# Cross attention with its softmax by blocks of 1024 keys, each block turned on TensorE and its two halves copied by ScalarE and VectorE

## What is computed

```python
x = x + _L0_xattn_ref(_layernorm(x, axis=-1), ctx_768, ctx_768, ...)
...
q = jnp.einsum('bqd,dh->bqh', query, Wq) + bq
k = jnp.einsum('bkd,dh->bkh', key, Wk) + bk
v = jnp.einsum('bkd,dh->bkh', value, Wv) + bv
scores = jnp.einsum('bqh,bkh->bqk', q, k)
weights = jax.nn.softmax(scores, axis=-1)
return jnp.einsum('bqk,bkh->bqh', weights, v)
```

```python
powers = jnp.exp(dtA[:, :, None] * jnp.arange(L))
K = 2.0 * jnp.einsum('dn,dnl->dl', dC, powers).real
```

## Time and profile before

| | us |
|---|---|
| median of 3 runs | 1661.75 (1659.3 to 1729.4) |
| the profiled execution | 1659.78 |
| its span | 1657.9 |
| mean granted TensorE clock | 0.933 of full speed |
| cross attention, first score pass to last output | 191.7 to 511.2 |

### The profile page before, as it was taken

One profiled execution on the slowest core, in us unless ns is written; L12 is line 12 of the kernel. 1 busy time (PEld: TensorE's weight loads), 2 busy tenths in 40 slices (PEclk: granted clock), 3 DMA queues, 4 the chain that ended last, 5 costly groups with the idle time before them and its releaser, 6 DMA issues. The chain is left out here.

```text
span 1657.9 us, 19830 instructions
## 1 busy us (share of the span) xinstructions
PE 1369.8 (83%) x6709; PEld 729.4 (44%) x6763; DVE 1255.7 (76%) x2833; ACT 897.2 (54%) x1424; POOL 678.3 (41%) x466
## 2 busy tenths in 40 slices
PE   6677699999997757889899988989875459999798
PEld 2223344333344434355555555555564323333465
DVE  5999567866515669999999999999878657776433
ACT  4666211457543320687778778877852146666311
POOL 2656111112101034688787878878861120000012
PEclk9799899999997878999999999999987759999899
DMA  6000011000005832000000000000040300000000
GB/s 152 1 0 1 28 58 49 0 1 0 1 0 125 174 103 63 1 1 1 1 1 1 1 1 1 1 1 1 7 152 1 89 1 1 1 1 1 1 0 14
DMA packets 32482, 42.99 MB, mean 26 GB/s; under 512 B 14286, under 2 KB 25644, under 8 KB 30992
## 3 DMA queue, kind: packets, MB, share of 16 engines
q1 hardware_dynamic: 29820, 29.61, 6.2%
q10 hardware_dynamic: 2552, 12.02, 3.5%
HBM read 33.48 MB, written 8.14 MB: 25 GB/s over the span
## 5 line engine op out<-in xcount | busy, mean ns | idle before, releaser
L1631 PE MATMUL psum<-film_ka,film_context_qa 97*128 97x427 bf16 (+3 forms) x896 | 329.8, 368 | 74.3 <-DVE film_stage_kept L1810 29.4
L2033 ACT ACTIVATE film_stage_e<-psum,film_stage_bias 128x512 f32<-128x512 f32 (+1 forms) x416 | 273.9, 668 | 96.9 <-PE psum L1633 87.0
L1810 DVE MAX8 film_stage_kept<-psum 128x8 f32<-128x213 f32 (+1 forms) x960 | 318.5, 377 | 6.6 <-PE psum L1633 6.3
L1633 PE MATMUL psum<-film_kb,film_context_qb 128*128 128x427 bf16 (+2 forms) x843 | 306.4, 364 | 0.0
L1882 POOL TENSOR_TENSOR film_stage_e<-film_stage_e 128x1024 f32<-128x1024 f32 (+1 forms) x91 | 207.1, 2276 | 80.7 <-DVE film_stage_e L1852 60.8
L1852 DVE SCALAR_TENSOR_TENSOR film_stage_e<-psum,film_context_top,film_stage_e 128x512 f32<-128x512 f32 (+1 forms) x325 | 231.8, 719 | 8.4 <-ACT film_stage_e L2033 6.7
L1631 PEld LDWEIGHTS psum<-film_ka,film_context_qa 97*128 97x128 bf16 x896 | 92.1, 103 | 195.3 <-DVE film_stage_kept L1810 86.8
L3235 POOL TENSOR_TENSOR residual<-residual,top_expert_kept 128x1024 f32<-128x1024 f32 x7 | 16.5, 2351 | 294.9 <-DVE top_expert_kept L3192 294.9
L1913 PEld LDWEIGHTS psum<-ctx_rows,film_stage_mean_T 128*128 128x128 f32 (+1 forms) x816 | 121.9, 192 | 30.0 <-issue 3.3
L2998 DVE TENSOR_REDUCE gqa_attend_low<-psum 128x1 f32<-128x128 f32 (+7 forms) x128 | 94.1, 755 | 43.1 <-PE psum L2917 40.7
L1913 PE MATMUL psum<-ctx_rows,film_stage_mean_T 128*128 128x96 f32 (+1 forms) x816 | 119.9, 269 | 1.8
(11 more groups left out here) (548 smaller groups left out, 2540.3 us busy)
## 6 DMA issues: line engine op xcount, KB each, us to landing
film_kb<-film_k_rows ACTq DMA_DIRECT2D x4, 1601.0 KB
film_ka<-film_k_rows ACTq DMA_DIRECT2D x3, 1601.0 KB
ctx_T<-in_ctx_T SPq DMA_DIRECT2D x1, 2401.5 KB
gqa_experts_w<-in_L_ffn_W SPq DMA_DIRECT2D x1, 2048.0 KB
film_stage_e<-in_dft_ahead SPq DMA_DIRECT2D x1, 1728.0 KB, 8.7
film_k_rows<-cross_attention_film_hi SPq DMA_DIRECT2D x6, 256.0 KB, 2.0
film_k_rows<-cross_attention_film_mid SPq DMA_DIRECT2D x6, 256.0 KB, 2.0
film_k_rows<-cross_attention_film_low SPq DMA_DIRECT2D x6, 256.0 KB, 2.0
```

The costliest lines, as they stand in the source:

```text
L1631: pe.matmul(out, a["qa"][0:ROWS, h, rows], a["ka"][0:ROWS, h, c + b:c + b + cols], start=True, stop=False)
L1633: last = pe.matmul(out, a["qb"][:, h, rows], a["kb"][:, h, c + b:c + b + cols], start=False, stop=True)
L1810: last = dve.max(kept[:, h % 2, PER_PIECE * u + s, :], bank[:, lo:hi])
L2033: act.activation(e[:, n % RING, sub, 0:PIECES[u][1]], ps[:, SEARCH_BANKS + q % WEIGH_BANKS, 0:PIECES[u][1]], ACT.Exp, bias=bias[:, i % 2, ...
```

## The change

The scores are formed once. For each block n = 7 i + c of 128 queries and 1024 keys, the loop over n (56 blocks and 4 iterations behind them) does this: TensorE forms the negative scores into one of two pairs of banks; VectorE takes their minimum per query; ScalarE takes exp(minimum - negative score) of 128x1024 into `prob`; two iterations later TensorE turns `prob` in two halves of four 128x128 tiles into banks 4 and 5; ScalarE copies the first half (h = 0) to `prob_T`, VectorE the second (h = 1); TensorE multiplies each turned tile as weights with 97 columns of `ctx_rows`, summed over the block in a place of its own in bank 6. The short block has a first half only. At the end of a row the seven minima give seven scales, and GpSimd scales and adds the seven sums. At the end the totals are turned and multiplied by `w_v` as before.

The S4D filter and the FiLM keys move into this loop. The FiLM keys are now 13 units of 512 columns, one in each iteration from 1 to 13, in bank 7 (`side`). The filter's small arithmetic is cut into parts 0 to 10, in the iterations 2 to 12 (`S4D_SMALL_AT`), the groups begin at iteration 12 (`S4D_FROM`), two of them every five iterations, and the filter's products, copies and turns use bank 7 too. The first loads of SyncE change places: those for keys and filter are issued ahead of the wait for `ones_set`.

In the diff below the helpers of the filter and the keys are left out; they are cut into pieces, but do the same operations, those of the keys on 512 columns.

```diff
+    LAG, PROBS, TURNED = 2, 3, 3
...
+    key_at = {KEYS_FIRST + u: u for u in range(len(KEY_UNITS))}
...
+    angles_at = {S4D_FROM + 5 * x // 4: divmod(x, 2) for x in range(2 * NG)}
+    pair_at = [S4D_FROM + 5 * p for p in range(NG // 2)]
+    scalar_at = {5: 1, 8: 2}
+    for p, n in enumerate(pair_at):
+        scalar_at[n + 4], scalar_at[n + 5] = 2 * p + 3, 2 * p + 4
+    decay_at = {n + 2 * b: 2 * p + b for p, n in enumerate(pair_at) for b in range(2)}
+    power_at = {n + 6 + b: 2 * p + b for p, n in enumerate(pair_at) for b in range(2)}
+    product_at = {n + 8 + b: 2 * p + b for p, n in enumerate(pair_at) for b in range(2)}
+    rows_at = {n + 10: p for p, n in enumerate(pair_at)}
...
+    END = max(BLOCKS + LAG + 2, max(kernel_at) + 1)
...
+    parts_at = {NB * i + FIRST_PART - 1 + LAG + 1: 2 * i for i in range(NT)}
+    parts_at.update({NB * (i + 1) - 1 + LAG + 1: 2 * i + 1 for i in range(NT)})
...
+            def bring_together(i):
+                pool.wait_ge(part_copied, 2 * i + 2)
+                pool.wait_ge(scale_ready, i + 1)
+                x = sums[:, i % 2]
+                link(pool.tensor_tensor(x, x, scale[:, i, :].unsqueeze(2).to_broadcast([P, NB, CA]), ALU.mult))
+                link(pool.tensor_tensor(x[:, 0:3], x[:, 0:3], x[:, 3:6], ALU.add))
+                link(pool.tensor_tensor(x[:, 0:2], x[:, 0:2], x[:, 2:7:4], ALU.add))
+                pool.tensor_tensor(total[:, i, :], x[:, 0], x[:, 1], ALU.add).then_inc(total_ready, 1)
...
+            def copy_turned(n, h):
+                k = half_at[n, h]
+                dve.wait_ge(turn_done, k + 1)
+                dve.tensor_copy(prob_T[:, k % TURNED, :], ps[:, 4 + k % 2, :]).then_inc(turned_high, 1)
...
+            for n in range(END):
+                if n in parts_at:
+                    copy_part(parts_at[n])
+                if n < BLOCKS:
+                    i, c = divmod(n, NB)
                     dve.wait_ge(score_done, n + 1)
...
-                    dve.reduce_max(tops[:, i, c:c + 1], pair(2 * (n % SCORE_PAIRS))[:, 0:width],
-                                   AX).then_inc(max_read, 1)
...
-            dve.wait_ge(max_read, NT * N_CHUNK)
-            link(dve.reduce_max(top[:], tops[:], AX))
-            dve.tensor_scalar(minus_top[:, :, DC], top[:], -1.0, None, ALU.mult).then_inc(top_ready, 1)
-            s4d_vector(dve, link, s4d, ps[:, 4, :])
...
+                    dve.tensor_reduce(shift[:, i, c:c + 1], scores(n), AX, ALU.min).then_inc(shift_ready, 1)
...
+                if (n - LAG, 1) in half_at:
+                    copy_turned(n - LAG, 1)
+                if n in key_at:
+                    film_key_vector(dve, film, side, key_at[n])
+                if n in small_at:
+                    s4d_vector_small(dve, link, s4d, side, small_at[n])
+                if n in angles_at:
+                    s4d_vector_angles(dve, link, s4d, *angles_at[n])
+                if n in power_at:
+                    s4d_vector_power(dve, s4d, power_at[n])
+            s4d_vector_skip(dve, link, s4d)
...
+            def turn(n, h):
+                k = half_at[n, h]
+                pe.wait_ge(prob_ready, n + 1)
+                if k >= 2:
+                    pe.wait_ge(*turned(k - 2))
+                for _, x, rows in key_tiles(n, h):
+                    last = pe.transpose(ps[0:rows, 4 + k % 2, x:x + P],
+                                        prob[:, n % PROBS, h * HALF + x:h * HALF + x + rows], g["ident"][:])
+                last.then_inc(turn_done, 1)
...
+            def weighted(n, h):
+                k = half_at[n, h]
...
+                pe.wait_ge(*turned(k))
+                if h == 0 and c in (0, FIRST_PART) and part >= 1:
+                    pe.wait_ge(part_copied, part)
+                for tile, x, rows in key_tiles(n, h):
+                    last = pe.matmul(ps[:, SUMS_BANK, place:place + CA], prob_T[0:rows, k % TURNED, x:x + P],
+                                     ctx[0:rows, tile, :], start=tile % 8 == 0,
+                                     stop=tile == min(8 * c + 7, KT - 1))
+                if (n, h + 1) not in half_at and c in (FIRST_PART - 1, NB - 1):
+                    last.then_inc(part_done, 1)
...
+            for n in range(END):
+                b = n - LAG
+                if 0 <= b < BLOCKS:
+                    turn(b, 0)
+                if 0 <= b - 1 < BLOCKS:
+                    weighted(*HALVES[half_at[b - 1, 0] + ((b - 1, 1) in half_at)])
+                if n < BLOCKS:
+                    i, c = divmod(n, NB)
+                    if n >= 2:
+                        pe.wait_ge(prob_ready, n - 1)
+                    for h in range(-(-width(n) // HALF)):
+                        cols = min(HALF, width(n) - h * HALF)
+                        last = pe.matmul(ps[:, 2 * (n % 2) + h, 0:cols], qc[:, i * P:(i + 1) * P],
+                                         ctx_T[:, c * CHUNK + h * HALF:c * CHUNK + h * HALF + cols],
+                                         start=True, stop=True)
+                    last.then_inc(score_done, 1)
+                if (b, 1) in half_at:
+                    turn(b, 1)
+                    weighted(b, 0)
+                if n in key_at:
+                    if key_at[n] == 0:
+                        pe.wait_ge(s4d["sem"]["zeroed"], 1)
+                    film_key_tensor(pe, film, ctx_T, side, key_at[n])
+                if n in product_at:
+                    if product_at[n] == 0:
+                        pe.wait_ge(film["sem"]["rest_ready"], len(KEY_UNITS))
+                    s4d_tensor(pe, s4d, side, product_at[n])
+                if n in turn_at:
+                    s4d_turn(pe, s4d, side, turn_at[n])
...
-            pe.wait_ge(shift_ready, 2)
...
-                for n in range(2):
-                    last = pe.matmul(ps[0:rows, 2 * (k % 2) + n, :], ctx_T[:, k * P:k * P + rows],
-                                     qc_shifted[:, n * HALF:(n + 1) * HALF], start=True, stop=True)
-                last.then_inc(prob_psum, 1)
-                if k >= 1:
-                    weighted(k - 1)
...
+            def copy_turned(n, h):
+                k = half_at[n, h]
+                act.wait_ge(turn_done, k + 1)
+                whole = sum(rows == P for _, _, rows in key_tiles(n, h)) * P
+                last = act.activation(prob_T[:, k % TURNED, 0:whole], ps[:, 4 + k % 2, 0:whole], ACT.Copy)
...
+            for n in range(END):
+                b = n - LAG
+                if (b, 0) in half_at:
+                    copy_turned(b, 0)
+                if n < BLOCKS:
+                    i, c = divmod(n, NB)
+                    act.wait_ge(shift_ready, n + 1)
+                    act.activation(prob[:, n % PROBS, 0:width(n)], scores(n), ACT.Exp, scale=-1.0,
+                                   bias=shift[:, i, c:c + 1]).then_inc(prob_ready, 1)
...
+                if n in key_at:
+                    film_key_high(act, film, side, key_at[n])
+                if n - 1 in key_at:
+                    film_key_middle(act, film, key_at[n - 1])
+                if n in scalar_at:
+                    s4d_scalar(act, s4d, scalar_at[n])
+                if n in rows_at:
+                    s4d_copy_rows(act, s4d, side, rows_at[n])
+                if n in kernel_at:
+                    s4d_copy_kernel(act, s4d, side, kernel_at[n])
+            for n in range(2):
```

More of the change, by code:

```diff
@@ L623, in s4d_vector, with s4d_vector_angles @@
+def s4d_vector_angles(dve, link, k, q, part):
+    sem = k["sem"]
+    b = q % RING_Q
+    group = slice(q * GROUP, (q + 1) * GROUP)
     i_index = k["index"][:, 0:P].unsqueeze(1).to_broadcast([P, GROUP, P])
-    for q in range(NG):
-        b = q % RING_Q
-        group = slice(q * GROUP, (q + 1) * GROUP)
+    if part == 0:
         if q >= RING_Q:
@@ L771, in film_key_store @@
     sem = f["sem"]
-    for u, (c, w) in enumerate(UNITS):
+    for u, (c, w) in enumerate(KEY_UNITS):
         for k, part in enumerate(("hi", "mid", "low")):
@@ L875, in cross_attention @@
     ctx_T = g["ctx_T"]
+    NB = N_CHUNK
+    BLOCKS = NT * NB
+    HALVES = [(n, h) for n in range(BLOCKS) for h in range(2) if h == 0 or n % NB < NB - 1]
+    half_at = {x: k for k, x in enumerate(HALVES)}
+    LAG, PROBS, TURNED = 2, 3, 3
+    FIRST_PART = 4
     w_q = m.sb("w_q", [P, D])
@@ new lines, in copy_part @@
+            def copy_part(part):
+                i = part // 2
+                blocks = part_blocks(part)
+                dve.wait_ge(part_done, part + 1)
+                if i >= 2:
+                    dve.wait_ge(total_ready, i - 1)
+                dve.tensor_copy(sums[:, i % 2, blocks[0]:blocks[-1] + 1, :],
+                                ps[:, SUMS_BANK, 0:len(blocks) * CA].rearrange("p (b c) -> p b c", c=CA)
+                                ).then_inc(part_copied, 1)
+            dve.memset(side, 0.0).then_inc(s4d["sem"]["zeroed"], 1)
@@ L1038, in _ @@
-            weighted(KT - 1)
-            pe.wait_ge(sum_ready, 1)
-            for i in range(NT):
```

(9 more changed lines are left out.)

425 lines of the change are left out of this document (200 added, 225 removed).

## The result

The changed kernel takes 1670.05 us (median of six runs, 1667.55 to 1672.61) where the kernel before takes 1661.97: ratio 1.0053, interval 1.0039 to 1.0067. It is 0.5% slower; I had forecast 0.8% less. The ratio leaves out one run of the kernel before (1729.4 us) that fell in the slower state of the chip. The profiled span went from 1657.9 to 1665.6 us. Where a place in a trace is compared between kernels, it is counted from the first reduction, which starts at 193.8 us here and between 193.2 and 197.3 in the traces of the experiments.

What follows compares the result with a forecast made beforehand. A ring through VectorE bounds the new loop, not TensorE's own work; 191.7 + 85 + 207 + 14 = 497.7 against 511.2, 13 us less, so 1649 us (-0.8%), range 1612 to 1680.

Steps and rivals of the forecast that it cites:

- The first 14 iterations: Iterations 0 to 13, which also carry the FiLM keys: 85 us, set by a round of 3.76 us plus small work.
- X: VectorE's small filter work added to the 3.76 us round in the first part: about 31 us with angles.
- port rival: GpSimd operations hold up VectorE's tensor_scalars: 39 us in all and 8 in the first part, kernel 1696; chance 0.06.
- The loop: Iterations 14 to 55, six rows: 34.5 us a row, of which 2.5 stick out of the ring's slack; 207 us.
- ScalarE's low copy: Iterations with sines and the next: copy delayed by 1.15 and 1.1 us, of which 0.65 and 0.6 are seen.
- The copy of the sums: VectorE's copies of the sums in each row: two copies, 0.3 us of a row's 32.
- the ring's idle 0.7: TensorE idle 0.7 us per full iteration (5.05 against 4.36 of work), covering 16 small filter matmuls of about 0.65.
- The end: Behind the last scores, through the last four of eight outputs (2.9 us): about 14 us, where 7.3 were.
- the ring through VectorE: Each score waits for VectorE's reduction, its high copy and that half's weighting: 5.05 us per full iteration.
- 41 and the turn: TensorE has 41 us less work in the sweeps, and the 5.1 us turn between them goes too.
- The clock: Rival: holes in each iteration lower TensorE's granted clock; at 0.85 28 us more, kernel 1677; chance 0.10.

Runs made afterwards that it cites:

- run 13: Changed kernel, but from the third key unit on GpSimd forms the low part of the keys on 8 columns, not 512: ratio 1.0005 to the kernel before.
- 9: Changed kernel, but GpSimd forms the decay of one channel in each group of eight, read by ScalarE for all eight: ratio 1.0023 to the kernel before.
- Runs 3: Changed kernel, with ScalarE's second filter step cut over two iterations, its exponential moved to the next: ratio 1.0067 to the kernel before.
- 10: Changed kernel, with sine and exponential of one index only in the filter's second step, table loads kept: ratio 1.0049 to the kernel before.
- run 6: Changed kernel, with VectorE also copying the low halves that ScalarE would copy behind its filter work (18 of 56): ratio 0.9996 to the kernel before.
- run 11: Changed kernel, with only two of the four key tiles in each full block's first half weighted: ratio 1.0012 to the kernel before.

## Why the prediction was wrong

**The step that failed** is the small work in "The first 14 iterations", 31 us for X: it measured 43.3 (38.6 and 4.7 of angles). I took it from a stretch of before in which the FiLM keys were done, and laid it beside GpSimd's low part, which I priced only as a store that is in time. I had its neighbour in hand: the earlier trace rows show the hold, and my port rival even wrote 8 us for the first part. But it was tied to the decays and given 0.06. The release decides: low part and small work are both freed within 0.05 us at the end of the same chain, so they meet in ten of thirteen units. By runs 13 and 9 the holds cost 8 us here and some 5 for the decays, where the rival had 39 for these: behind the power that frees a decay, a reduction and a copy out of PSUM come first in VectorE's queue, as at 317.4 and 344.4, and cover most of its 1.90 us. The Trainium skill ("SBUF — State Buffer", SBUF: two separate sides) tells of an exclusive lock; the held operations of run 13 and the unchanged reductions agree.

That 12.3 us of excess in X equal the first part's 12.2 is partly luck: with 8.6 of small work gone, run 13's first part is only 7.4 shorter.

**The other 4 to 5 us of the first part** hold the rest of the small work's excess, the second step (7.8 us waited), a sums copy behind VectorE's work (7.3), and the half clock behind these waits (about 5 us by the estimate above, so some other term must have been too long). Runs 3 and 10 show that shortening the step alone brings nothing, so its hole is not a separate price. I can't split it further.

**The loop**, 6.6 us. A row with nothing on top would be 3.43 + 6 x 4.79 = 32.2; I had 32. On top I had 2.5 a row, 14.6 us in 41 iterations; it is 20.1. Three terms were too small. ScalarE's low copy: I had 1.25 in five iterations, some 10, and TensorE waits 13.9, behind table load, two sines and the exponential in ScalarE's queue; run 6 gives back 9.5. The copy of the sums: I had 0.3 a row, and TensorE waits 5.2. The iterations with the filter's products, which I had called covered by the ring's idle 0.7: about 2, by run 11. The decays' hold, which I had at nothing, is in there too.

**The end**: all eight outputs come behind the last total, not four, since TensorE turns every total first: 5.5 us (514.81 to 520.35) in place of 2.9. The granted clock is 0.50 there, but it was low in the like stretch of before too (0.65 from 505 to 511.2), so it is no part of the miss. The other 1.2 us lie ahead of the outputs; no run splits them.

**Right**: the ring through VectorE as the order of a clean iteration (run 11). TensorE's tiles cost what I had. But the ring holds by 0.3, not by 0.7, since I had it 0.27 too long; that a row of 32 us came out (32.2) all the same, with clean iterations of 4.79 and not 5.05, is luck. TensorE's busy time fell by 22 us (1369.8 to 1347.9), where I had 41 and the turn. The Trainium skill's drain behind a table load ("ScalarE: Activation LUTs", What ACT_TABLE_LOAD costs) is not seen here either: the sine at 305.77 starts 1.30 us after its load, at 304.47.

**The clock** was a rival at 0.10, with a sign: below 0.95 in the stage. The stage has 0.94 (before: 0.98), so the sign came. The loop, for which it was priced, has 0.98, though 0.50 from 411 to 414. The low clock lies in the first part (0.87) and the outputs, each time behind a wait, so I take it for a follow-up of the waits; no run changes it by itself.

## What to carry to other kernels

When a change brings two streams together, price VectorE's operations on SBUF by who is released at the same moment: a GpSimd operation that starts first holds them for nearly its whole length, and one chain that frees both makes that happen nearly every time. Ask of each copy on the path not how long it is but what stands ahead of it in its queue in the worst iteration, and give it to the engine whose queue is short just then; here that, with the keys' remainder one iteration later, turned 0.5% slower into 0.5% faster. Shortening the largest hole can bring nothing when the next wait behind it takes over.

## What I had not expected of the hardware

- A GpSimd tensor_tensor of 1.16 us adds 0.96 to a VectorE operation on SBUF that starts 0.05 later, whether that takes 0.23 or 2.30 alone; reductions and copies out of PSUM stay at 1.22 and 0.68.
- After waits of 7.3 and 7.8 us, the next eight f32 passes of 97 columns took 2.00 and 2.02 us; at full clock 1.13. At 410.9 the same happened after a wait of 1.96, while at 360.5, after one of 2.05, they took 1.13.
- Eight f32 passes of 97 columns (four products) push the next matmul back by 0.87 us when they follow without a wait, about what the earlier trace rows give (0.105 a pass), and by 0.97 behind a wait or ahead of the filter's products; four transposes by 0.43 to 0.49.
